# A blockwise scan on one core: four passes over a block for six, each with a second pass over a guess of the errors

## The reference

```
k, v   = split(layernorm(x) @ W_KV)
params = (W1, b1, W2, b2)
for t in 0..1023:                                  # both sequences share params
    g = grad(mean((silu(k_t @ W1 + b1) @ W2 + b2 - v_t) ** 2))
    params -= 0.001 * g
x += silu(q @ W1 + b1) @ W2 + b2                   # q = layernorm(x) @ W_Q, last params
```

## Time and profile before

| | us |
|---|---|
| median of 3 runs | 555.06 |
| lowest and highest | 549.68, 557.04 |
| span of the profiled execution | 530.0 |
| of it: up to the first steps of the scan | 0 to 162.4 |
| first steps | 162.4 to 181.2 |
| turns 0 to 15 | 181.2 to 373 |
| query, output rows, second expert layer | 373 to 530 |

### The profile page before, as it was taken

How to read it: one execution, slowest core, us unless ns; L and a number is a source line. 1 busy time by engine, 2 the same in 40 slices (tenths; PEclk the granted TensorE clock), 3 DMA queues, 4 the chain that set the end, 5 groups by cost and what they waited for, 6 DMA issues and landing times.

```text
span 530.0 us, 10763 instructions
## 1 busy us (share of the span) xinstructions
PE 468.9 (88%) x3167; PEld 390.3 (74%) x3167; DVE 321.6 (61%) x1252; ACT 261.1 (49%) x697; POOL 248.5 (47%) x367
## 2 busy tenths in 40 slices
PE   7998899999099899999999999999998959999950
PEld 6443799999046698888888888887464449999950
DVE  4855455554394577787778877774497524545523
ACT  2782455555104445555555555553478525555530
POOL 3177775445102225555454455553204777655440
PEclk9799999999779889999999999997989989999985
DMA  8962361000661000000000000000000133400009
GB/s 228 258 226 55 105 192 40 29 30 13 172 166 31 1 2 0 2 2 1 2 1 2 1 2 0 2 2 2 1 2 25 52 106 105 138 29 28 28 21 231
DMA packets 34518, 30.95 MB, mean 58 GB/s; under 512 B 3838, under 2 KB 30085, under 8 KB 34464
## 3 DMA queue, kind: packets, MB, share of 16 engines
q1 hardware_dynamic: 24608, 19.17, 13.7%
q0 software_dynamic: 4544, 8.47, 4.9%
q10 hardware_dynamic: 5312, 2.62, 1.9%
HBM read 15.55 MB, written 15.61 MB: 59 GB/s over the span
## 4 chain that ended last, share of the span: by engine, by line
PE 67%; DVE 11%; ACT 6%; DMA 6%; POOL 5%; issue 4%; ACTq 0%; DVEq 0%; SPq 0%; POOLq 0%
PE bank L1150 16%; PE bank L703 14%; PE bank L690 13%; PE bank L651 4%; PE bank L561 4%; POOL slots_dram L1275 2%; DMA stage<-y_dram 2%; PE bank L661 2%; PE bank L1044 2%; ACT ahead_a L1096 2%; PE bank L678 2%; PE bank L1046 1%; PE bank L580 1%; DMA stage<-slots_dram 1%; ACT sq L1097 1%
## 5 line engine op out<-in xcount | busy, mean ns | idle before, releaser
L1492 DVE TENSOR_TENSOR sq<-bank,relu 128x512 f32<-128x512 f32 x86 | 59.5, 691 | 88.8 <-ACT relu L803 88.6
L1280 POOL DMA_INDIRECT y_dram<-y_out,stage x78 | 76.6, 981 | 60.3 <-ACT y_out L829 53.8
L1275 POOL DMA_INDIRECT slots_dram<-rows,slots x64 | 63.1, 986 | 55.6 <-ACT rows L754 27.4
L703 PE MATMUL bank<-proj_w,sq 128*128 x624 | 86.5, 282 | 2.7 <-DVE sq L1492 2.7
L690 PE MATMUL bank<-tileT,tile_w 128*128 128x128 f32 x624 | 83.3, 278 | 0.0
L703 PEld LDWEIGHTS bank<-proj_w,sq 128*128 128x128 f32 x624 | 75.7, 191 | 6.3 <-issue 3.5
L803 ACT ACTIVATE relu<-bank 128x512 f32<-128x512 f32 x94 | 56.0, 596 | 46.1 <-PE bank L690 37.7
L690 PEld LDWEIGHTS bank<-tileT,tile_w 128*128 128x128 f32 x624 | 77.0, 195 | 0.0
L829 ACT ACTIVATE y_out<-bank,stage 128x128 f32<-128x128 f32 x78 | 28.7, 368 | 33.2 <-PE bank L703 33.2
L561 PE MATMUL bank<-ones 128*128 128x512 f32 x38 | 23.6, 772 | 15.3 <-DVE res L1543 12.5
L651 PE MATMUL bank<-ln_t,fc_w 128*128 128x512 f32 x64 | 33.6, 622 | 0.0
(11 more groups left out here) (283 smaller groups left out, 1234.4 us busy)
## 6 DMA issues: line engine op xcount, KB each, us to landing
slots_dram<-pad SPq DMA_DIRECT2D x2, 2535.0 KB, 14.9
stage<-slots_dram SPq DMA_DIRECT2D x18, 260.0 KB, 4.5
fc_w<-experts SPq DMA_DIRECT2D x1, 2048.0 KB, 21.7
proj_w<-experts SPq DMA_DIRECT2D x1, 2048.0 KB, 25.1
stage<-y_dram SPq DMA_DIRECT2D x8, 256.0 KB, 5.4
stage<-y_dram ACTq DMA_DIRECT2D x8, 256.0 KB, 6.2
y_dram<-y_out,stage POOLq DMA_INDIRECT x78, 2.3
res<-x SPq DMA_DIRECT2D x4, 256.0 KB, 4.1
```

Source lines behind the costliest of these rows:

```text
L703: last = nc.tensor.matmul(bank[4 + i % 2][:, 0:P], sq[:, i % 2, f_cols], proj_w[:, k, f_cols], start=j == 0, stop=j == FJ - 1)
L1275: nc.gpsimd.indirect_dma_start(to, bass.IndirectOffsetOnAxis(slots[:, n:n + 1], 0), rows[:, k, b, :], None, bounds_check=limit, oob_is_err ...
L1280: nc.gpsimd.indirect_dma_start(y_dram.ap(), bass.IndirectOffsetOnAxis(tiles[:, t, P:P + 1].bitcast(U32), 0), y_out[:, t % YBUFS, :], None, ...
L1492: nc.vector.tensor_tensor(wide_of(i)[2], wide_of(i)[0][:], wide_of(i)[1], ALU.mult)\
```

## The change

A late step and an early step are now both *two* passes over the errors. TensorE first computes a guess of the errors in row layout: offset (b2 - v, transposed by `ident_r`), plus the old guess, plus a W2 (`pe_offset`, `pe_old_guess`, `pe_yrows`); ScalarE copies it to `guess`; then y = W2 a + (guess)(a a) (`pe_y`, `pe_inner`) takes the guess in place of the old e. The last late step (`inner` false) has no guess and takes the old e as before (`pe_y_old`, `pe_y_last`). ROUNDS and AHEAD go from 3 to 2, FIRST_AHEAD from 4 to 3. The chain `mid` is gone: both late steps are `final`, in fp32. The orders of TensorE, VectorE and ScalarE are written out anew, and the parameters are made in another order, w1 first. TOL goes from 3e-5 to 5e-5. The wait counters of the key parts are merged into one (`key_multiplied`), with 5 parts per first step.

```
-AHEAD = 3
-ROUNDS = 3
-FIRST_AHEAD = 4
+AHEAD = 2
+ROUNDS = 2
+FIRST_AHEAD = 3
...
-TOL = 3e-5
+TOL = 5e-5
...
+        START_PARAMS = ("ident_r", "b1_half", "ahead_w1", "ahead_b1_half", "ahead_b1", "ahead_w2", "ahead_b2", "ahead_w2t")
+        PARAMS = ("w1", "b2", "b1", "b1_half", "ahead_w1", "w2t", "w2", "ahead_b1", "ahead_b1_half",
+                  "ahead_w2t", "ahead_b2", "ahead_w2")
+        LAST_PARAMS = ("w1", "b2", "b1", "b1_half", "w2t", "w2")
...
-            earlier = Step(ahead, n - 1, n - 1, turn, 2)
+            earlier = Step(ahead, n - 1, n - 1, turn, 1 + (turn + 1) % 2)
             late, early = [], []
             for r in range(ROUNDS):
-                late.append(Step(final if r else mid, ROUNDS * turn + r, (ROUNDS - 1) * turn + r, turn, r,
-                                 late[-1] if r else earlier, r < ROUNDS - 1))
-                early.append(Step(ahead, n + r, n + r, turn + 1, r, early[-1] if r else None))
+                late.append(Step(final, ROUNDS * turn + r, turn + r, turn, r, late[-1] if r else earlier, r == 0))
+                early.append(Step(ahead, n + r, n + r, turn + 1, 1 + turn % 2 if r else 0, early[-1] if r else None))
...
...
+        def wait_param(eng, step, turn, name):
+            if is_fresh(step) and (step.chain is ahead or turn):
+                eng.wait_ge(params_done, params_at(turn, ("ahead_" if step.chain is ahead else "") + name))
+        def pe_first(pe, step, turn):
+            x = step.chain
+            if step.n:
+                pe.wait_ge(x.th_done, step.n)
+            wait_param(pe, step, turn, "w1")
+            ins = mm(x.h_bank, x.w1, x.k[:, col(step.block)], stop=step.old is None)
+            if step.old is None:
+                ins.then_inc(x.h_done, 1)
+        def pe_again(pe, step):
             x, old = step.chain, step.old
+            pe.wait_ge(old.chain.d_done, old.n + 1)
+            mm(x.h_bank, old.chain.ed[:, old.to, 1, :], old.chain.kk[:, step.block, :], start=False)\
+              .then_inc(x.h_done, 1)
+        def pe_offset(pe, step, turn):
+            x = step.chain
+            pe.wait_ge(offset_done, 2 * step.block + (1 if x is ahead else 2))
+            if step.n:
+                pe.wait_ge(x.d_done, step.n)
+            wait_param(pe, step, turn, "b1_half" if x is ahead else "w1")
+            mm(x.d_bank, x.offset, ident_r[:], stop=False)
+        def pe_old_guess(pe, step):
             x, old = step.chain, step.old
+            pe.wait_ge(old.chain.erows_done, old.n + 1)
+            pe.wait_ge(old.chain.aa_done, old.m + 1)
+            mm(x.d_bank, old.chain.aa[:, old.to, :], old.chain.ed[:, old.to, 0, :], start=False, stop=False)
+        def pe_yrows(pe, step, turn):
+            x = step.chain
+            pe.wait_ge(x.a_done, step.n + 1)
+            wait_param(pe, step, turn, "w2")
+            mm(x.d_bank, x.a, x.w2, start=False).then_inc(x.yrows_done, 1)
+        def pe_aa(pe, step, turn):
+            x = step.chain
+            pe.wait_ge(x.a_done, step.n + 1)
             if step.m:
                 pe.wait_ge(x.ee_done, step.m)
+            if x is final:
+                wait_param(pe, step, turn, "b1_half")
+            nc.tensor.matmul(x.y_bank[:, P:2 * P], x.a, x.a, start=True, stop=True)
+        def pe_y(pe, step, turn):
+            x = step.chain
+            wait_param(pe, step, turn, "w2")
+            mm(x.y_bank, x.w2, x.a, stop=False).then_inc(x.aa_mm, 1)
+        def pe_inner(pe, step):
+            x = step.chain
+            pe.wait_ge(x.aa_done, step.m + 1)
+            pe.wait_ge(x.guess_done, step.m + 1)
+            mm(x.y_bank, x.guess, x.aa[:, step.to, :], start=False).then_inc(x.y_done, 1)
+        def pe_y_old(pe, step):
+            x, old = step.chain, step.old
+            pe.wait_ge(x.ee_done, old.m + 1)
+            pe.wait_ge(x.erows_done, old.n + 1)
+            mm(x.y_bank, x.ed[:, old.to, 0, :], x.aa[:, old.to, :], stop=False)
             pe.wait_ge(x.a_done, step.n + 1)
+        def pe_y_last(pe, step):
+            x = step.chain
+            mm(x.y_bank, x.w2, x.a, start=False).then_inc(x.y_done, 1)
+        def pe_a_transposed(pe, step, turn):
+            x = step.chain
+            pe.wait_ge(x.a_done, step.n + 1)
             if step.n:
                 pe.wait_ge(x.erows_done, step.n)
+            wait_param(pe, step, turn, "w2")
             nc.tensor.transpose(x.t_bank[:, 0:P], x.a.bitcast(F32), ident[:])
+        def pe_th_transposed(pe, step):
+            x = step.chain
             pe.wait_ge(x.th_done, step.n + 1)
             nc.tensor.transpose(x.t_bank[:, P:2 * P], x.th, ident[:]).then_inc(x.t_done, 1)
+        def pe_da_old(pe, step):
+            x, old = step.chain, step.old
+            pe.wait_ge(x.rows_done, step.n + 1)
+            pe.wait_ge(old.chain.ee_done, old.m + 1)
+            if step.inner:
+                pe.wait_ge(x.guess_done, step.m + 1)
+            else:
+                pe.wait_ge(x.d_done, step.n)
+            mm(x.d_bank, as_kind(step, old.chain.ee[:, old.to, :]), x.rows[:, 0:P], stop=False)
         def pe_da(pe, step):
+            x = step.chain
             pe.wait_ge(x.e_done, step.n + 1)
+            mm(x.d_bank, x.e, x.w2t, start=step.old is None).then_inc(x.da_done, 1)
+        def pe_ee(pe, step):
+            x = step.chain
+            pe.wait_ge(x.e_done, step.n + 1)
+            nc.tensor.matmul(x.y_bank[:, 2 * P:3 * P], x.e, x.e, start=True, stop=True).then_inc(x.ee_mm, 1)
+        def pe_e_transposed(pe, step):
+            x = step.chain
             pe.wait_ge(x.u_done, step.n + 1)
+            pe.wait_ge(x.e_done, step.n + 1)
             nc.tensor.transpose(x.t_bank[:, 2 * P:3 * P], x.e.bitcast(F32), ident[:]).then_inc(x.et_done, 1)
+        def pe_w1_sums(pe, step, done):
+            x = step.chain
             pe.wait_ge(x.d_done, step.n + 1)
+            weights = mm(x.d_bank, k_rows[:, step.block, :], x.ed[:, step.to, 1, :].bitcast(F32))
             if x is final:
                 weights.then_inc(done, 1)
+        def pe_b1_sums(pe, step, done):
+            x = step.chain
+            if x is ahead:
+                pe.wait_ge(x.d_done, step.n + 1)
+            nc.tensor.matmul(bias_bank(x)[:, P:P + 2], x.ed[:, step.to, 1, :], x.rows[:, P:P + 2], start=True,
+                             stop=True).then_inc(done, 1)
+        def pe_w2_sums(pe, step):
+            x = step.chain
+            pe.wait_ge(x.erows_done, step.n + 1)
+            mm(x.t_bank, x.rows[:, 0:P], x.ed[:, step.to, 0, :])
+        def pe_w2t_sums(pe, step, done):
+            x = step.chain
+            nc.tensor.matmul(x.t_bank[:, P:2 * P + 2], x.ed[:, step.to, 0, :], x.rows[:], start=True, stop=True)\
               .then_inc(done, 1)
...
+        def act_offset(act, step, turn):
+            x = step.chain
+            if x is ahead or turn:
+                act.wait_ge(params_done, params_at(turn, "ahead_b2" if x is ahead else "b2"))
+            nc.scalar.activation(x.offset, v_t[:, col(step.block)], ACT.Identity, bias=x.b2, scale=-1.0)\
+              .then_inc(offset_done, 1)
...
+        def act_guess(act, step):
+            x = step.chain
+            act.wait_ge(x.yrows_done, step.m + 1)
+            nc.scalar.copy(x.guess, x.d_bank[:, 0:P]).then_inc(x.guess_done, 1)
...
+        def dve_aa(dve, step):
+            x = step.chain
+            dve.wait_ge(x.aa_mm, step.m + 1)
+            nc.vector.scalar_tensor_tensor(x.aa[:, step.to, :], x.y_bank[:, P:2 * P], 1.0, mask, ALU.add,
+                                           ALU.mult).then_inc(x.aa_done, 1)
...
             for turn in range(NBLK):
                 late, early = turn_steps(turn)
+                dve_aa(dve, late[0])
+                dve_u(dve, late[0])
+                dve_e(dve, late[0], turn)
+                if early:
+                    dve_aa(dve, early[0])
+                dve_d(dve, late[0])
+                if early:
+                    dve_u(dve, early[0])
+                    dve_e(dve, early[0], turn)
+                dve_ee(dve, late[0])
+                if early:
+                    dve_d(dve, early[0])
+                    dve_ee(dve, early[0])
+                dve_e(dve, late[1], turn)
+                dve_u(dve, late[1])
+                if early:
+                    dve_aa(dve, early[1])
+                dve_d(dve, late[1])
+                if early:
+                    dve_u(dve, early[1])
+                    dve_e(dve, early[1], turn)
+                dve_w1(turn)
+                if early:
+                    dve_d(dve, early[1])
+                more = turn < NBLK - 2
+                dve_biases(turn)
+                if more:
+                    dve_ahead_w1(turn)
+                dve_w2()
+                if more:
+                    dve_ahead_b1(turn)
+                if early:
+                    dve_ee(dve, early[1])
+                if more:
+                    dve_ahead_w2(turn)
...
             for turn in range(NBLK):
```

(95 more changed lines are left out.)

373 lines of the change are left out of this document (159 added, 214 removed).

## The result

The new kernel takes **515.23 us** (median of 4 runs, 513.47 to 517.95), the kernel before in the same job 553.31 (549.68 to 557.04): ratio **0.9331**, 95% interval [0.9262, 0.9399], so 6.7% faster. The forecast was 521 in a range from 508 to 538. The profiled execution took 513.47 us, 1.9 above its span.

The account below looks back on a forecast made before the run. The turn was taken as bounded by TensorE's in-order stream and, at its joint, by hops between engines. Gains of 27.3, 2.0, 3.0, 1.0 and 0.4 gave 33.7, taken from 555.1 for about 521 us, range 508 to 538.

Parts of the forecast that it names:

- The timetable: One new turn placed from measured hops: 9.65 us, 8.5 passes and 1.15 standstill; 9.8 taken to allow for small waits.
- the wait ahead of first(E0): At the turn's joint, TensorE waits for VectorE's ahead w1; as a sign, the longest idle of TensorE.
- more standstill: Rival: about ten waits in the turn each 0.1 late, turn 10.8, 536 us; chance 0.23.
- the stream alone: Rival: E's work fills everything, turn 8.5 plus the ahead w1 wait, 8.9, 508 us; chance 0.14.
- Turns 1 to 14: Full scan turns: each falls from 11.76 to 9.8 us, 14 x 1.95 = 27.3 gained.
- Turn 0: First scan turn with its joint, 13.50 us with a slow-clock stretch: gain 2.0, as a full turn.
- Turn 15: Last turn, only late steps: 12.92 to 9.9 us, including 1.3 for low clock, gain 3.0.
- First steps: Steps ahead of the turns: four in 18.80 us become three in 17.8, gain 1.0; bounds 4.7 gain to 0.7 loss.
- turns 0 to 15 in some 160 us: Sign that the forecast is right: the whole scan's turns together take some 160 us.
- the base: Starting time of the sum: 555.1 us, the median of the runs, 25.1 above the profile's span, carried over.
- The clock rival: Rival: TensorE's clock drops to 1.2 GHz in the turns; with half of them low 577 us; chance 0.05.
- The guard: Rival: gap exceeds 5e-5 and 1024 serial steps of at least 4.0 us follow, about 4,600 us; chance 0.03.

Follow-up runs that it names:

- The six extra passes: New kernel with the first product of every step in the turns issued twice: 519.42 us, ratio 0.9468; a turn 10.04 against 9.54.
- the moved first(E0): New kernel with first(E0) moved on TensorE from ahead of the old guess of L0 to behind y(L0): 521.56 us, ratio 0.9519.
- two rounds and no second pass: Kernel before with ROUNDS and AHEAD at 2, one pass per step, gap set to zero and TOL 1e3: 501.09 us, ratio 0.9129.
- the ten runs: Kernel before, unchanged, run again for a second profile in the second job: 549.14 us.
- The first profile of before: Kernel before, unchanged, the profile the prediction was made from: span 530.0 us, timed runs 549.7 to 557.0.
- fillings elsewhere: Kernel before with unread products of ones on TensorE, in the last turn or ahead of or behind turn 0's sums: 548.9, 552.66 and 549.72 us.
- the third profile: Kernel before, unchanged, profiled again after the filling experiments: 552.07 us, beside 552.39.
- that whole profile: New kernel with TOL back at 3e-5 in place of 5e-5, so the serial branch was taken: 9143.81 us in one run.

## Why the prediction was right, and where its terms were off

**What bounds the turn: right.** The timetable agrees with the trace within 0.1 us at three places of the joint and four of the body, and its turn of 9.65 was nearer than the 9.8 taken: the 0.15 for small waits did not come. 75 x 0.113 = 8.5 of 9.56 is passes and 1.1 standstill, where 1.15 was placed. The six extra passes show that the stream sets most of the turn, the moved first(E0) that one wait of E's ahead of L's inner product costs half a microsecond. One sign was wrong: the wait ahead of first(E0), 0.2, is not the turn's longest. The load of da(E0) comes 0.46 behind the pair before it (264.38 and 263.92), where a pair takes 0.22, so 0.24 is waited for e(E0).

**Passes: right.** 13 fewer, 88 to 75. The fall of the turn from 11.76 to 9.56 is 1.5 us of passes and 0.7 of standstill. The rivals of more standstill (10.8) and of the stream alone (8.9) both failed on the turn. Standstill there is, 2.2 us a turn, with two rounds and no second pass; that the second pass's own products fill it fits the sums but was not shown by itself.

**The terms**, compared at the full clock, since the new kernel had it:

- Turns 1 to 14: 164.69 to 133.87, a gain of 30.8 where 27.3 was summed. This is the term that was mis-sized: 0.25 us in each of 14 turns, of which 0.15 is the allowance for small waits and 0.1 the timetable.
- Turn 0: 11.1 to 9.2, a gain of 1.9, as the 2.0 of the sum. My base of 13.50 was a draw with the slow clock.
- Turn 15: 10.83 to 8.03, a gain of 2.8 where 3.0 was. Both of my ends were too high (12.92 and 9.9), the one by a draw, the other by the 1.3 that I added for a slow clock.
- First steps: 18.8 to 17.3, a gain of 1.5 where 1.0 was.
- The end: from the last subtraction to the product with w1 1.19 us before and 0.88 now, a gain of 0.3 where 0.4 was.

Without the end that is 37.0, and the two scans, 205.3 and 168.4, show 36.9. The medians gained 38.1 in the first job and 35.6 in the second (36.5 by the ten runs). The first profile of before, whose scan had both slow stretches, made it look like 41.5. The sign "turns 0 to 15 in some 160 us" came out as 151.1. By the terms of the sum it was 158.6 (137.2, 11.5 and 9.9); of the 7.5 us between, 3.3 are turns 1 to 14 and 4.2 are turns 0 and 15, mostly the slow stretches that I left in them. Of the 6.2 us between 521.4 and 515.23, 4.4 is the sum and 1.8 the base, whose median of three runs was 555.06 and of four 553.31.

**The step that was wrong in kind** is the base. I put 25.1 us "around the span" on top of a profile. A run is its span and about 1.9 us, in every run on record. The work outside the scan took 320.1 us in the one profile that I had, and 339.2 to 346.1 in the twelve others, of both kernels and their variants. The forecast did not suffer because its total came from the median and only differences came from the profile: that is luck in so far as the 25.1 stood for something else than was thought, and would have been wrong on any other base. What makes that part vary was not found, but the traces show where it lies. In the expert layers VectorE waits for up to 6.2 us where the profile shows nothing ahead of it; two such waits of the new kernel:

```profile
387.91 0.69 DVE L1600 TENSOR_TENSOR stage<-bank,stage 128x512 f32<-128x512 f32 x1 [5.24 <-issue]
394.33 0.69 DVE L1600 TENSOR_TENSOR sq<-bank,relu 128x512 f32<-128x512 f32 x1 [5.73 <-issue]
```

The kernel before has them too (its line is L1492), here in the third profile, summed over the span (us in total, times, longest):

```profile
DVE stage L1492 <- issue: 15.2, 3, 6.2
...
DVE sq L1492 <- issue: 6.6, 2, 5.7
```

The first profile has none of them. All of VectorE's waits ahead of this line sum to 99.6 us there, to 123.8 in the third and 121.2 in the new kernel's first, which is about the 20 to 25 us in question.

**The clock rival: did not come.** In seven profiles of before (three of them with fillings elsewhere) no turn from 1 to 14 is longer than 11.95 us, in two of the new kernel none is longer than 9.80; a slow stretch of the size of turn 0's (2.4 us) is in none of them. What I read from the earlier trace rows, a clock that VectorE's hold-up and a lone chain had brought down, was one draw of several. The Trainium skill (TensorE: Matmul & The Clock Gate, A second HAM failure mode) tells of small idles between groups of matmuls that came with a swinging clock. The traces agree in part: idles and a slow stretch met in turn 0 (1.04 us ahead of it) and in the last turn, but the same idles brought none in other executions, and turns 2 to 14 of before, in which TensorE waited 0.5 us a turn for silu of E0 (6.6 us in 13 turns), kept their length throughout.

**The guard: nearer and dearer than I had it.** It was given 0.03 and 4 ms. It did not fire, but the gap is over 3e-5, and when it fires it costs 8.6 ms: a step takes 8.41 us, not 4.0. The 4.0 was a floor of nine hops priced at the higher clock, and the branch ran at the lower one; how much of the difference is the clock and how much are hops left out was not separated.

## What to carry to other kernels

When an in-order engine is shared by two dependent chains, place one whole turn in time from measured hops and count its passes beside it: the placing gave the turn to 0.1 us, and neither "so many passes fewer" nor "the stream alone" did. Work added inside a chain that waits can cost less than its stream (17 passes of 0.113 for 0.7 us), so a second correction within an iteration can pay for whole iterations, if the guard still holds. On an engine that works in order, moving a product that waits only moves the wait onto whatever then stands behind it. Before a slow-clock stretch, or a stage's length, enters a sum or an explanation, look at the same stretch in several profiles of the same kernel: two of mine were single draws, and an experiment seemed to confirm a cause until its untouched turns were read too.

## What the runs showed of the hardware that was not expected

- The granted clock of one short stretch differs between executions of the same program: turn 0 of the kernel before had a mean of 0.75 or 1.00 with about the same idle ahead of it (1.04 and 1.05 us in the slow ones, 1.04 to 1.14 in the others) and the same 81 passes in it.
- The serial branch, whose TensorE is busy 63% of the time, stayed at the lower level for 8.6 ms. The granted clock of that whole profile, in 40 slices:

```profile
PEclk9755555555555555555555555555555555555557
```

- A lone chain need not be slow: the last turn of the two-round kernel above, busy 5.60 of 7.50 us, had 1.00.
